# Attention of a transformer layer on one Trainium2 core: value products as column halves, row sums as column quarters, steps in blocks of two

## The reference, cut to what matters

```python
q = (x @ Wq + bq).reshape(Bv, Tv, N_HEAD, HEAD_DIM)
k = (x @ Wk + bk).reshape(Bv, Tv, N_HEAD, LATENT)
v = (x @ Wv + bv).reshape(Bv, Tv, N_HEAD, LATENT)
qc = jnp.einsum('bthd,dl->bthl', q, Wc)
att = jnp.einsum('bthl,bshl->bhts', qc, k) * SCALE
att = jnp.where(causal[None, None], att, -jnp.inf)
att = jax.nn.softmax(att, axis=-1)
y = jnp.einsum('bhts,bshl->bthl', att, v).reshape(Bv, Tv, N_HEAD * LATENT)
return y @ Wo + bo
```

## Time and profile before

| | us |
|---|---|
| median of three executions | 1122.53 |
| the three executions | 1125.27, 1122.53, 1118.86 |
| the profiled execution, whole | 1125.98 |
| its span, first to last instruction | 1124.2 |

### The profile page before, as it was taken

The page is one execution under the profiler, slowest core; times in us unless marked ns, Lnnn a source line. Parts: engine busy times, 40 slices in busy tenths (PEclk is TensorE's granted clock), DMA queues, the critical chain, the costliest instruction groups (busy, mean ns, idle before and its releaser), DMA issues.

```text
span 1124.2 us, 16448 instructions
## 1 busy us (share of the span) xinstructions
PE 904.0 (80%) x5179; PEld 734.7 (65%) x5179; DVE 569.0 (51%) x1644; ACT 409.8 (36%) x809; POOL 330.6 (29%) x326
## 2 busy tenths in 40 slices
PE   2306599999379889999999799599999937999983
PEld 2204276777237778988886688488888725777663
DVE  8431144444356776665652676267446514444443
ACT  1100122222144555555642455346435522222223
POOL 1736515555400000000000014531000262455551
PEclk9998799999779999999999899799999978999996
DMA  9800225444252021223120021210202102444525
GB/s 344 284 23 28 62 67 151 146 154 147 93 196 58 19 48 29 48 83 106 25 53 10 1 61 48 79 42 21 56 10 48 44 25 58 136 135 149 158 92 190
DMA packets 97475, 99.09 MB, mean 88 GB/s; under 512 B 15225, under 2 KB 82699, under 8 KB 96646
## 3 DMA queue, kind: packets, MB, share of 16 engines
q1 hardware_dynamic: 88198, 85.98, 25.7%
q0 software_dynamic: 9216, 12.33, 3.5%
HBM read 58.62 MB, written 38.60 MB: 86 GB/s over the span
## 4 chain that ended last, share of the span: by engine, by line
PE 56%; DVE 15%; another core or an unknown queue 12%; issue 10%; ACT 3%; DMA 2%; POOL 1%; SPq 1%; DVEq 0%; POOLq 0%; ACTq 0%
PE PS L1593 19%; PE PS L1551 6%; PE PS L1472 5%; PE PS L1576 5%; PE PS L1473 4%; DVE mxp L1167 3%; PE PS L1485 2%; PE PS L1639 2%; PE PS L1493 2%; DVE xs L1149 1%; ACT area_o L741 1%; PE PS L1554 1%; DMA yg<-ybuf 1%; PE PS L1579 1%
## 5 line engine op out<-in xcount | busy, mean ns | idle before, releaser
L1593 PE MATMUL PS<-pT,area_v 128*128 128x256 f32 (+1 forms) x1280 | 305.2, 362 | 4.8 <-ACT area_o L779 4.8
L1167 DVE TENSOR_REDUCE mxp<-PS 128x2 f32<-128x512 f32 (+1 forms) x320 | 197.0, 630 | 139.9 <-PE PS L1551 67.0
L820 ACT ACTIVATE pT<-PS 128x512 f32<-128x512 f32 (+1 forms) x320 | 176.6, 553 | 235.8 <-PE PS L1579 113.9
L1593 PEld LDWEIGHTS PS<-pT,area_v 128*128 128x128 f32 x1280 | 213.9, 194 | 19.0 <-ACT area_o L779 5.1
L657 POOL DMA_INDIRECT ybuf<-area_o,yidx x160 | 155.4, 971 | 162.8 <-DVE area_o L1126 78.4
L643 POOL TENSOR_TENSOR area_o<-area_o,rden 128x512 f32<-128x512 f32 x31 | 39.5, 1273 | 494.0 <-DMA rden<-den 493.7
L1551 PE MATMUL PS<-Kz,Qx 128*128 128x256 f32 (+1 forms) x640 | 168.6, 356 | 18.6 <-DVE mxp L1167 11.3
L613 POOL DMA_INDIRECT xbuf<-xn,sidx x128 | 124.9, 976 | 112.5 <-issue 59.8
L1576 PE MATMUL PS<-Qx,Kz 128*128 128x256 f32 (+1 forms) x640 | 144.0, 307 | 5.4 <-ACT pT L820 2.3
L1551 PEld LDWEIGHTS PS<-Kz,Qx 128*128 128x128 f32 x640 | 113.8, 197 | 40.8 <-DVE mxp L1167 16.0
L1472 PE MATMUL PS<-area_o,area_v 128*128 128x320 f32 x256 | 97.3, 462 | 22.4 <-ACT area_o L741 17.4
(11 more groups left out here) (174 smaller groups left out, 898.5 us busy)
## 6 DMA issues: line engine op xcount, KB each, us to landing
area_v<-xbuf SPq DMA_DIRECT2D x32, 340.0 KB, 3.3
area_v<-in_L_ffn_wg_dram SPq DMA_DIRECT2D x32, 256.0 KB
area_v<-in_L_ffn_wu_dram SPq DMA_DIRECT2D x32, 256.0 KB
area_v<-in_L_ffn_wd_dram SPq DMA_DIRECT2D x64, 128.0 KB
rden<-den SPq DMA_DIRECT2D x248, 32.0 KB
yg<-ybuf SPq DMA_DIRECT2D x24, 256.0 KB, 4.6
qkbuf<-stage SPq DMA_DIRECT2D x24, 256.0 KB, 3.7
xbuf<-Kz SPq DMA_DIRECT2D x4, 1360.0 KB, 12.3
```

Source lines behind the costliest of these rows:

```text
L820: nc.scalar.activation(pT[:, N % 4, 0:w], PS[:, 2 + N % 2, 0:w], ACT.Exp).then_inc(exp_done, 1)
L1167: nc.vector.tensor_reduce(mxp[:, i, c, 2 * hp:2 * hp + 2], PS[:, k % 2, 0:2 * w].rearrange("p (h w) -> p h w", h=2), AX.X, ALU.max).then_i ...
L1593: ins = mm(PS[:, pv_bank(U, a), (p + 1) * TC - w:(p + 1) * TC], value_and_ones(j, h), pT[:, N % 4, a * w:(a + 1) * w], start=(N in UNIT_FI ...
```

## The change

Values and ones are no longer one set of weights. `pv(N)` now has, for each of the two heads, a product with the 64 value columns alone; the first head goes to partitions 0 to 63, the second to 64 to 127 of one bank. The sums get products of their own: `p_sums` has four of them, with 32 columns of ones as weights, one for each head of two steps, each to its quarter of the partitions of another bank. The steps go in blocks of two: scores of both, masks of both, row items of both, and then the values and the sums of the block before. On ACT, one copy of 128 partitions takes the place of the four that fetched a unit's sums, and one that of the two that fetched its values. The `memset` of the ones on POOL is gone.

```diff
-                for a in range(2):
-                    hh = 2 * p + a
-                    ins = nc.scalar.activation(den[U % 2][RW * hh:RW * hh + RW, :],
-                                               PS[LAT * (1 - a):LAT * (1 - a) + RW, pv_bank(U, a), TC * p:TC * p + TC], ACT.Copy)
-                ins.then_inc(den_ready, 1)
+                nc.scalar.activation(den[U % 2][:], PS[:, den_bank(U), 0:TC], ACT.Copy).then_inc(den_ready, 1)
...
                 for a in range(2):
                     h = VISITS[v][1] * HG + 2 * p + a
-                    ins = mm(PS[:, pv_bank(U, a), (p + 1) * TC - w:(p + 1) * TC], value_and_ones(j, h), pT[:, N % 4, a * w:(a + 1) * w],
-                             start=(N in UNIT_FIRST), stop=(j == 0), skip_group_check=True)
-                ins.then_inc(pv_done, 1)
+                    mm(PS[LAT * a:LAT * a + LAT, pv_bank(U), (p + 1) * TC - w:(p + 1) * TC], vs[:, j, h * LAT:(h + 1) * LAT],
+                       pT[:, N % 4, a * w:(a + 1) * w], start=(N in UNIT_FIRST), stop=(j == 0), skip_group_check=True)
+
+            def p_sums(N):
+
+                v, c, j, p = STEPS[N]
+                w = step_width(N)
+                for hh in range(HG):
+                    ins = mm(PS[RW * hh:RW * hh + RW, den_bank(UNIT_OF[N]), TC - w:TC], cst[:, C_ONE:C_ONE + RW],
+                             pT[:, (N - 1 + hh // 2) % 4, hh % 2 * w:(hh % 2 + 1) * w],
+                             start=(N - 1 in UNIT_FIRST), stop=(j == 0), skip_group_check=True)
+                ins.then_inc(pv_done, 2)
 
             def heads(b):
                 steps = steps_of(b)
-                for N in steps:
-                    s_cols(N)
-                    if N - LAG in steps:
-                        pv(N - LAG)
-                    for k in rows_at(N):
-                        row_item(k)
-                for N in steps[-LAG:]:
-                    pv(N)
+                for N in steps[::2]:
+                    two = (N, N + 1)
+                    for n in two:
+                        s_cols(n)
+                    if N in DIAG:
+                        for n in two:
+                            s_mask(n)
+                    for n in two:
+                        for k in rows_at(n):
+                            row_item(k)
+                    if N > steps[0]:
+                        two_pv(N - 2)
+                two_pv(steps[-2])
+
+            def two_pv(N):
+                pv(N)
+                pv(N + 1)
+                p_sums(N + 1)
```

More of the change, by code:

```diff
@@ L61 @@
 R0 = RW - 3 * HD
-VP = 3 * LAT
 SCALE = 1.0 / 8.0
@@ L196, in loads, with pv_bank, den_bank, s_bank @@
     return sum(u <= v and u % 2 == v % 2 for u in LOADED)
-def pv_bank(U, a):
-    return 4 + 2 * (U % 2) + a
+def pv_bank(U):
+    return 5 + 2 * (U % 2)
+def den_bank(U):
+    return 4 + 2 * (U % 2)
+def s_bank(N):
+    return 2 + N % 2
 def score_bank(f):
@@ L664, in _ @@
             results(0)
-            nc.gpsimd.memset(vs[:, :, :, 1, :], 1.0).then_inc(v_ones, 1)
             for b in range(B):
@@ L761, in high_part, with sums_out @@
                 nc.scalar.activation(stage[n % 2][0][:], PS[:, k % 2, :], ACT.Identity, bias=qkb[:, q:q + 1]).then_inc(high_ready, 1)
-            def sums(U, p):
+            def sums_out(U):
                 act.wait_ge(pv_done, UNIT_STEP[U] + 1)
@@ L767, in sums, with latents @@
                     act.wait_ge(rep_done[U % 2], 16 * 2 * HG * (U // 2))
-                for a in range(2):
-                    hh = 2 * p + a
-                    ins = nc.scalar.activation(den[U % 2][RW * hh:RW * hh + RW, :],
-                                               PS[LAT * (1 - a):LAT * (1 - a) + RW, pv_bank(U, a), TC * p:TC * p + TC], ACT.Copy)
-                ins.then_inc(den_ready, 1)
-            def latents(U, a):
+                nc.scalar.activation(den[U % 2][:], PS[:, den_bank(U), 0:TC], ACT.Copy).then_inc(den_ready, 1)
+            def latents(U):
                 g, c = VISITS[UNITS[U][0]][1], UNITS[U][1]
                 act.wait_ge(pv_done, UNIT_STEP[U] + 1)
-                lanes = slice(LAT * a, LAT * a + LAT)
-                nc.scalar.activation(yT[lanes, 2 * g:2 * g + 2, c * TC:(c + 1) * TC],
-                                     PS[lanes, pv_bank(U, a), :].rearrange("p (c t) -> p c t", c=2), ACT.Copy).then_inc(y_free, 1)
+                nc.scalar.activation(yT[:, 2 * g:2 * g + 2, c * TC:(c + 1) * TC],
+                                     PS[:, pv_bank(U), :].rearrange("p (c t) -> p c t", c=2), ACT.Copy).then_inc(y_free, 1)
             def unit_out(step, b):
-                for part in range(4):
+                for part, evacuate in enumerate((sums_out, latents)):
                     for U in units_at(step, EVAC + part, b):
[L785 to L788, removed]
+                        evacuate(U)
             def values(b, tiles):
@@ L818, in heads @@
                     if N >= 4:
-                        act.wait_ge(pv_done, N - 3)
-                    nc.scalar.activation(pT[:, N % 4, 0:w], PS[:, 2 + N % 2, 0:w], ACT.Exp).then_inc(exp_done, 1)
+                        act.wait_ge(pv_done, N // 2 * 2 - 2)
+                    nc.scalar.activation(pT[:, N % 4, 0:w], PS[:, s_bank(N), 0:w], ACT.Exp).then_inc(exp_done, 1)
                     unit_out(N, b)
@@ L1575, in s_cols, with s_mask @@
                 for a in range(2):
-                    ins = mm(PS[:, 2 + N % 2, a * w:(a + 1) * w], Kz[v % 2][:, 2 * p + a, j * P:(j + 1) * P],
+                    ins = mm(PS[:, s_bank(N), a * w:(a + 1) * w], Kz[v % 2][:, 2 * p + a, j * P:(j + 1) * P],
                              Qx[v % 2][:, t1 - w:t1], start=(a == 0), stop=N not in DIAG, skip_group_check=True)
[L1578 to L1581, removed]
+                if N not in DIAG:
+                    ins.then_inc(st_ready, 1)
+            def s_mask(N):
+                w = step_width(N)
+                mm(PS[:, s_bank(N), 0:2 * w].rearrange("p (h w) -> p h w", h=2)[:, :, 0:P], causS[:],
+                   identb[:].unsqueeze(1).broadcast_to([P, 2, P]), start=False, stop=True, skip_group_check=True).then_inc(st_ready, 1)
             def pv(N):
```

32 lines of the change are left out of this document (13 added, 19 removed).

## The result

| | before | after |
|---|---|---|
| median, us | 1121.09 (4 runs, 1118.86 to 1125.27) | 1179.61 (4 runs, 1176.00 to 1182.15) |
| profiled execution, us (its span) | 1125.98 (1124.2) | 1181.04 (1179.2) |
| ratio after / before | | 1.0507, interval 1.0483 to 1.0531 |

What follows compares the result with a forecast made beforehand. PE's stream of turns was taken to bound attention. Shapes net of saved turns added 7 us and waits at row items 43: 1122.5 + 50 = 1172.5, say 1172; forecast 1145 to 1197 (62%), 8 in 10 within 1125 to 1210.

Steps and rivals of the forecast that it cites:

- The bound: In both attention stretches PE's stream of turns sets the time; ACT's copies, 54 us less, count nothing.
- Turns of halves and quarters: Values and sums in attention: halves run two at a time, quarters four, 6 turns a wide block, saving 67.6 us.
- Quarters two at a time: Rival for the sums products: quarters overlap only in pairs, two turns more a block, 61 us, 1233; 8%.
- Changes of shape: Three changes of array shape in each of 160 attention blocks cost PE 0.465 us a block, 74 us.
- Cheap switches: Rival: shape changes cost 0 in a dense stream, giving 1098; faster if below 0.16 us a block; 13%.
- The gaps at R items: PE idles behind DVE's maximum at a block's third row item, 0.80 us: 32 us, plus 5 for longer blocks.
- No gaps: Rival: shapes cost as forecast, but PE does not idle on row items because DVE keeps up, 1129.5; 9%.
- The gap before T items: At 10 blocks a T item directly follows its unit's last R item; PE idles 1.7 us, 10 us more altogether.
- 7 + 43: Attention total: 7 us longer from shape changes less saved turns, and 43 us of PE idle at moved row items.
- The cover of the exponentials: PE work hiding ACT's exponentials in a block: thin only in narrow blocks; without it each could lose 0.2 us.
- The clock: Rival: gaps lower PE's clock to 1.2 GHz for a tenth of attention, some 25 us, 1197 and up; 8%.

Runs made afterwards that it cites:

- the version with the order alone: Kernel before with blocks of two in the new order, ACT's copies following in two steps, values and ones still 128 columns: 1082.47 us, ratio 1.0519.
- the version with the values as quarters: Changed kernel with four value products of 32 columns a step instead of two of 64: 1072.85 us, ratio 1.0416.
- split rows: Changed kernel with row items of a block's second step behind the block's values and sums: 1054.95 us (1.0241), on another chip 1142.28 us (1.0222).
- version with both edits: Changed kernel with row items of the second step behind values and sums, and values as four products of 32 columns: 1035.43 us, ratio 1.0052.

## Why the prediction held, point by point

**The bound.** Right. ACT's load fell and the kernel didn't gain by it; every edit that took time out of PE's stream in attention showed up in the total. In blocks of two ACT's separate copies would count: 5.9 us in the version with the order alone.

**Turns of halves and quarters.** Right, with the forecast's choice for the quarters: four at a time, 2 turns a block. *Quarters two at a time* (1233) falls with the 0.64 us of the sums group. A turn in the dense stream is 0.216, though, as one of a full product, not the 0.21 I had from `replicate`: 6 of them are 0.04 more. "TensorE: Matmul & The Clock Gate" of the Trainium skill, section "Measured speedup vs the span model", had spoken for less than full overlap; the trace doesn't agree with it here. By that ratio, as an estimate, a turn of four quarters would be 0.27 us; in the version with the values as quarters the second four start 0.24 after the first and every further four 0.216.

**Changes of shape.** Predicted 0.465 a block, measured 0.49. Into halves 0.14 (forecast 0.15), back to 128 columns 0.22 (0.195), and halves to quarters, which no row of before had, 0.12, just what I took between 0 and 0.15. The choice had a reason, the same 0.09 and half the load, and the parts are 0.10 and 0.02; that it hit is in part luck. The rule of the Trainium skill's "TensorEngine Tiling (Array Packing)", section "Key Properties", is that a change of mode drains the engine. The trace agrees that each change costs time, and between halves and quarters too. In wide blocks I had saving and price cancel to nothing and the trace has 0.05 lost, 6 us in 128 blocks; in narrow ones I had 0.22 lost, and a narrow block takes 2.32 against 2.18 in the version with the order alone, 0.14, so 4.5 in 32. Together 11 us, forecast 7. *Cheap switches* (1098) needed less than 0.16 us a block and falls by a factor of three.

**The gaps at R items.** The mechanism and its size are right: 0.80 us forecast, 0.81 in the block shown, and 50 waits at the weight load, 0.77 each, where I had said some 50 of 0.7. *No gaps* (1129.5) falls: DVE is idle for 110 of 267 us in the first stretch, and PE waits for it all the same. The list of PE's waits counts only 0.55 of each, because a matmul's modelled end lies behind its turn; the block lengths tell the whole.

**The gap before T items.** 1.7 forecast, 1.70 at the load, and the list has 17.5 us instead of 7.3: 10.2 more, forecast 10.

**What is over.** The sum was 7 + 43, and 58.5, 66.3 and 63.6 us were measured in three groups. If for each block the shortest of the three profiles of the changed kernel is taken, and of the kernel before too, the difference is 53.1 us (an estimate of what an undisturbed pair would show): 27.8 in the 36 blocks with three or more row items and no T, 20.5 in the 26 with a T, 3.8 in the others outside steps 200 to 219, and 1.0 in these. Less the 11 us of shapes that is 42 for the gaps, forecast 43. So the forecast's terms hold nearly in full, shapes 4 us too small; and the 5 to 13 us above the 53 lie in blocks that took longer in one profile than in another. The cover of the exponentials, which I had called thin in narrow blocks only and put at nothing, was too small for the order alone with ACT's separate copies (5.9 us in seven blocks, five of them wide blocks with two R items), but not for the changed kernel, which has no such wait in these five.

**The clock.** This rival didn't decide, but it may hold what is left. In one block of the changed kernel PE stood idle for 1.74 us, and what follows runs at the lower level:

```profile
412.24 0.50 PE L1543 MATMUL PS<-Kz,Qx 128*128 128x256 f32 x2 [1.74 <-DVE mxp L1159]
412.67 1.94 PE L1589 MATMUL PS<-pT,area_v 128*64 128x256 f32 x8
414.54 1.08 PE L1597 MATMUL PS<-pT,cst 128*32 128x256 f32 x8
```

The halves take 1.94 instead of 1.08, the quarters 1.08 instead of 0.64: 1.2 instead of 2.4 GHz. If for each piece of 5 us of the two attention stretches the missing share of the clock is multiplied by its length, three profiles of the kernel before have 12 to 17 us, and three of the changed one 22, 27 and 34. That bounds the clock's part from above, since some of it falls on idle time: by group, at most 5 of the 58.5, 22 of the 66.3 and 15 of the 63.6. The two stand in the same order, which fits the clock, but three pairs don't show it. The measure falls with the waits: from 27 to 22 us where the rows are split, and from 20 to 12 where they are split beside the quarters, so that up to 5 of those 35.7 us and 9 of those 37.4 may be clock that came back. In the version with the order alone it is 10, no more than before, so its waits cost what they cost without it. How large the clock's part of the last 5 to 13 us is stays open.

## What to carry over

Price a change of the array's shape like an instruction: here 0.11 to 0.22 us each, against 0.216 for a matmul of 256 columns, so dividing the array pays only if many products of one shape stand in a row. Before an order is coarsened, look for the pairs that hand a buffer to another engine and back; each needs other work between them, here 0.8 us at a third item and 1.7 at a reduction's end, even when that other engine is idle for 40% of the time. Copies that were free under one order need not be under another. And read such waits from the lengths of whole blocks, not from the list of waits alone.

## What was not expected of the hardware

**A kernel's time differs between the groups by 84 us, and it is not TensorE's clock.** The kernel before took 1029.8 us in one group and 1114 to 1121 in the others; each of the three groups ran on a chip of its own. The trace of the second group's kernel before up to its first score, and of the first group's version with both edits (the same work up to there):

```profile
0.00:340.60 340.60, 218.18 (x1029) 153.58 (x1030) 148.46 (x570) 71.61 (x135) 150.72 (x151) 0.93 0.45 144
```

```profile
0.00:299.10 299.10, 208.23 (x1028) 150.62 (x1029) 148.20 (x570) 71.66 (x135) 147.82 (x150) 0.93 0.52 165
```

The mean clock is the same. So is the time for which the DMA engines were busy, 0.45 x 340.6 = 153 and 0.52 x 299.1 = 156 us: the transfers are not slower, they stand still for longer. The longer stretch has two waits of DVE that the other has not:

```profile
71.16 0.22 DVE L979 TENSOR_TENSOR yg<-PS,rn 128x64 f32<-128x64 f32 x1 [29.14 <-remote]
103.51 0.23 DVE L914 TENSOR_SCALAR wq<-pT 128x128 f32<-128x128 f32 x1 [16.46 <-remote]
```

"remote" is what the profile says where it can't name who ended a wait. The two make 45.6 us. Another 18 us are in attention's second stretch, at steps 200 to 219: 44 to 51 us in all ten profiles of the slower chips, 28 to 31 in the four of the fast one, and there ACT and DVE wait for "remote" too. At both places POOL issues its indirect DMAs of `xbuf`. What these waits are for is open. On the slower chips every version has them, so the ratios hardly feel it: split rows have 1.0222 and 1.0241.

**Four quarters share the array without loss.** Eight matmuls of 256 columns on four quarters take the time of two and the latency, and 16 with different weights (1.07 us) that of four.

**The price of a change of shape has two parts.** At each change some 0.1 us goes (0.09 to 0.11, from 128, 64 or 32 columns to another), and the turn behind it is longer, by 0.02 us where the new weights have 32 columns, 0.05 with 64 and 0.10 with 128. So it is above all the number of changes that counts, and then how wide the shape is that one goes to.
